# A ring of 24 row slots instead of 16 in both expert passes of a cross-attention and expert-FFN kernel

## The reference

```python
# attention without softmax: 16 heads of 16
kv  = einsum('bthd,bthe->bhde', k, v)          # k, v from the context
att = einsum('bqhd,bhde->bqhe', q, kv) * scale # q from layernorm(x)
x   = x + layer_norm(att + layernorm(x)) * gamma + beta
# expert layer: two of 16 experts per token
t        = layernorm(x)
weights  = softmax(t @ gate_w.T)
w2, idx2 = top_k(weights, 2)
y        = relu(einsum('nh,edh->ned', t, expert_w) + expert_b)
out      = x + sum(y[idx2] * w2)
```

## Time and profile before

| | us |
|---|---|
| time, median of 3 runs | 858.72 (858.34 to 859.48) |
| the profiled execution's own time | 860.73 |
| its span | 859.0 |
| dense half and sorting table, to the first load of pass 0 | 0 to 458.8 |
| pass 0, first to last scatter started | 465.5 to 655.9 |
| pass 1, first to last scatter started | 666.6 to 850.6 |
| end of the span | 859.0 |

### The profile page before, as it was taken

How to read it: one execution, slowest core, us unless ns; L and a number is a source line. 1 busy time by engine, 2 the same in 40 slices (tenths; PEclk the granted TensorE clock), 3 DMA queues, 4 the chain that set the end, 5 groups by cost and what they waited for, 6 DMA issues and landing times. The chain is left out here.

```text
span 859.0 us, 21023 instructions
## 1 busy us (share of the span) xinstructions
PE 752.7 (88%) x5501; PEld 656.9 (76%) x5502; DVE 670.9 (78%) x2218; ACT 593.4 (69%) x1683; POOL 594.6 (69%) x783
## 2 busy tenths in 40 slices
PE   8999999999999999999998777777868799778850
PEld 5887888888888888888875777777765799777740
DVE  5999999999999999999985857777763566555540
ACT  5987999998999999989962545555542577545530
POOL 5575767777777777666663767777674677777774
PEclk9999999999999999999999989999999999999985
DMA  7699988999998877776414889999886999999942
GB/s 200 148 245 309 253 256 246 273 256 251 249 263 249 247 234 224 230 232 224 151 52 152 289 279 304 314 316 310 296 298 224 339 391 385 318 305 321 304 155 73
DMA packets 142885, 218.33 MB, mean 254 GB/s; under 512 B 39103, under 2 KB 74431, under 8 KB 142807
## 3 DMA queue, kind: packets, MB, share of 16 engines
q1 hardware_dynamic: 112999, 131.21, 48.1%
q0 software_dynamic: 29808, 86.20, 32.7%
HBM read 96.36 MB, written 116.80 MB: 248 GB/s over the span
## 5 line engine op out<-in xcount | busy, mean ns | idle before, releaser
L663 POOL DMA_INDIRECT bins<-row_in,put_at x143 | 139.2, 973 | 61.3 <-issue 48.3
L635 POOL DMA_INDIRECT bins<-rows x128 | 130.4, 1019 | 70.6 <-POOL rows L628 47.9
L663 POOL DMA_INDIRECT out_rows<-xh,put_at x143 | 138.9, 971 | 55.8 <-issue 39.4
L742 PE MATMUL ps_q<-h_t,wq 128*128 128x256 f32 x512 | 131.6, 379 | 1.3 <-ACT h_t L970 1.3
L742 PEld LDWEIGHTS ps_q<-h_t,wq 128*128 128x128 f32 x512 | 91.6, 189 | 14.6 <-ACT h_t L970 1.8
L1029 ACT ACTIVATE ps_q<-ps_q,row_in 128x256 f32<-128x256 f32 x144 | 58.6, 445 | 57.2 <-PE ps_q L856 56.7
L854 PE MATMUL ps_q<-we_head,row_head 128*128 x288 | 88.1, 306 | 7.8 <-DVE row_rest L1321 7.8
L537 POOL TENSOR_TENSOR c_rest<-c_sb,c_head 128x240 fp32r<-128x240 f32 x64 | 48.2, 753 | 61.9 <-DVE x L1183 57.3
L612 POOL TENSOR_TENSOR x_beta<-xh,beta_sb 128x512 f32<-128x512 f32 x64 | 85.6, 1338 | 0.8 <-DVE x L1183 0.8
L855 PE MATMUL ps_q<-we_head,row_rest 128*128 x288 | 82.0, 285 | 0.0
L856 PE MATMUL ps_q<-we,row_head 128*128 x288 | 81.9, 285 | 0.0
(11 more groups left out here) (174 smaller groups left out, 2403.2 us busy)
## 6 DMA issues: line engine op xcount, KB each, us to landing
bins<-zeros SPq DMA_DIRECT2D x48, 768.0 KB, 4.6
row_in<-bins SPq DMA_DIRECT2D x128, 260.0 KB
row_in<-bins SPq DMA_DIRECT2D x160, 132.0 KB, 2.1
xh<-in_x SPq DMA_DIRECT2D x64, 256.0 KB, 4.7
c_sb<-in_ctx_t SPq DMA_DIRECT2D x64, 120.0 KB, 4.4
we<-in_we_t SPq DMA_DIRECT2D x8, 512.0 KB, 5.5
we<-be_dram POOLq DMA_DIRECT2D x8, 512.0 KB, 7.8
we<-row_in POOLq DMA_DIRECT2D x8, 512.0 KB, 6.5
```

Of the source, the lines that this page charges most:

```text
L635: pool.indirect_dma_start(out=bins[0], in_=r[:, t, :], out_offset=bass.IndirectOffsetOnAxis(ap=r[:, t, POS_COL:POS_COL + 1].bitcast(I32), ...
L663: pool.indirect_dma_start(out=bins[1] if k == 0 else out, in_=row_in[:, t, :] if k == 0 else y[:, t, :], out_offset=bass.IndirectOffsetOnA ...
L742: mm = pe.matmul(ps_q[dc][:, 0:S], wq[:, c, dc * P:(dc + 1) * P], h_t[:, c, :, :], start=(c == 0), stop=(c == KC - 1))
```

## The change

V goes from 16 to 24, so that a pass has 6 trips instead of 9. `row_in` and `y` have 24 slots each. The room comes from the dense half: `x_sb`, `h`, `x_beta` and `x1` become views of `y`, and `wkv_head` and `wkv_rest` views of `row_head` and `row_rest`, which only the expert passes use. With 12 pairs in a trip there are more scatter semaphores, so others are given up: the expert weights are counted on 2 semaphores instead of 8, and only the first 4 pairs of pass 1 come in two loads, with 4 semaphores. The table's two rows of 128 numbers meet inside the last trip (tiles 120 to 143), so its read is in two instructions. Of the first trip of pass 0, V // 4 is now 6: the first table read is of 6 numbers, the second of 18.

```diff
--- before.py
+++ after.py
@@ -47,7 +47,7 @@
 DUMP = TILES * P
 
 LEAD, FILLS, FACTS = 12, 48, 8
-V = 16
+V = 24
 PAIRS = V // 2
 FILL = TILES // FILLS
 TRIPS = TILES // V
@@ -60,6 +60,7 @@
 SUM_STEP = SLABS + 2
 FIRST_FOLD, FOLD_STEPS = SUM_STEP + 2, 3
 FIRST_HEAD = FIRST_FOLD + FOLD_STEPS
+SPLIT_PAIRS = 4
 RB = 4
 LOG_EXP_SET = 6
 
@@ -139,10 +140,12 @@
 
     def read(k, i, count=V):
 
-        half = int(isinstance(i, int) and i * V >= P)
-        row = (column * 2 + k) * 2 + half
         low = V - count if count > V // 2 else 0
-        eng.load(regs[low:low + count], table[row:row + 1, bass.ds(i * V - half * P + low, count)])
+        cut = min(max(P - i * V - low, 0), count) if isinstance(i, int) else count
+        for half, part in enumerate((slice(low, low + cut), slice(low + cut, low + count))):
+            row = (column * 2 + k) * 2 + half
+            if part.stop > part.start:
+                eng.load(regs[part], table[row:row + 1, bass.ds(i * V - half * P + part.start, part.stop - part.start)])
         return [nc.snap(r, min_val=0, max_val=max_val) for r in regs[low:low + count]]
 
     return read
@@ -178,8 +181,6 @@
         bin_base = sb("bin_base", [P, NT, 2, E])
         base_less = sb("base_less", [P, 2, E])
         eps = sb("eps", [P, 1])
-        wkv_head = sb("wkv_head", [P, KC, 2 * D], F32R)
-        wkv_rest = sb("wkv_rest", [P, KC, 2 * D], F32R)
         wq = sb("wq", [P, KC, D])
         wg = sb("wg", [P, KC, E])
         wg_centred = sb("wg_centred", [P, KC, E])
@@ -198,8 +199,10 @@
         pad_facts = sb("pad_facts", [P, 2, E, ROW - D])
 
 
-        xh = sb("xh", [P, 2, 4 * NT, D])
-        x_sb, h = [xh[:, n].rearrange("p (b t) d -> p b t d", t=NT) for n in range(2)]
+        y = sb("y", [P, V, D])
+        x_sb, h = [y[:, 4 * NT * n:4 * NT * (n + 1)].rearrange("p (b t) d -> p b t d", t=NT) for n in range(2)]
+        x_beta, x1 = [y[:, 8 * NT + 2 * NT * n:8 * NT + 2 * NT * (n + 1)].rearrange("p (b t) d -> p b t d", t=NT)
+                      for n in range(2)]
         c_sb = sb("c_sb", [P, 4, KC, SC])
         c_head = sb("c_head", [P, 2, KC, SC], F32R)
         c_rest = sb("c_rest", [P, 2, KC, SC], F32R)
@@ -209,8 +212,6 @@
         kvm = sb("kvm", [P, KC, P])
         att = sb("att", [P, NT, D])
         scaled = sb("scaled", [P, NT, D])
-        x_beta = sb("x_beta", [P, 2, NT, D])
-        x1 = sb("x1", [P, 2, NT, D])
         rows = sb("rows", [P, 4, NT, ROW])
         h2_t = sb("h2_t", [P, KC, NT, P])
         st = sb("st", [P, 3, 2, NT, 3])
@@ -253,7 +254,8 @@
         put_at = sb("put_at", [P, V], I32)
         row_head = sb("row_head", [P, RB, 2, KC, P], F32R)
         row_rest = sb("row_rest", [P, RB, 2, KC, P], F32R)
-        y = xh[:].rearrange("p a t d -> p (a t) d")[:, 0:V]
+        wkv_head, wkv_rest = [b[:].rearrange("p b t c n -> p (b t c n)")[:, 0:KC * 2 * D]
+                              .rearrange("p (c n) -> p c n", c=KC) for b in (row_head, row_rest)]
 
         ps_ht = ps("ps_ht", [P, KC, NT, P])
         ps_kv = ps("ps_kv", [P, 2 * D])
@@ -281,7 +283,7 @@
         s_wg = sem("gate_weights_loaded")
         s_ident = sem("identity_made")
         s_mask = sem("head_mask_made")
-        s_we = [sem(f"expert_weights_loaded{n}") for n in range(WE_PIECES)]
+        s_we = [sem(f"expert_weight_half{n}_loaded") for n in range(2)]
         s_whead = sem("weight_heads_ready")
         s_wminus = sem("weight_heads_negated")
         s_wrest = sem("weight_rests_ready")
@@ -365,7 +367,7 @@
         s_py = sem("pair_multiplied")
         s_y = sem("pair_result_ready")
         s_loc = sem("second_position_step")
-        s_part = [sem(f"partial_sums_loaded{n}") for n in range(PAIRS)]
+        s_part = [sem(f"partial_sums_loaded{n}") for n in range(SPLIT_PAIRS)]
         s_sum2 = sem("pair_rows_summed")
         s_put = [sem(f"pair_rows_put{n}") for n in range(PAIRS)]
 
@@ -425,7 +427,7 @@
                 for n in pieces(step - 4, 1):
                     sp.dma_start(we[:, :, piece(n)],
                                  we_t.rearrange("(c p) n -> p c n", p=P)[:, :, piece(n)]
-                                 ).then_inc(s_we[n], 16)
+                                 ).then_inc(s_we[n // (WE_PIECES // 2)], 16)
                 if step >= LEAD - 4:
 
                     sp.wait_ge(s_const, 2)
@@ -495,10 +497,12 @@
                     for j in range(PAIRS):
                         sp.wait_ge(s_put[j], put_count(1, 0, j))
                     load_part(0, D, FULL, s_in[0])
-                    for j in range(1, PAIRS):
+                    for j in range(1, SPLIT_PAIRS):
                         load_part(j, D, FULL, s_in[j])
                         load_part(j - 1, 0, D, s_part[j - 1])
-                    load_part(PAIRS - 1, 0, D, s_part[PAIRS - 1])
+                    load_part(SPLIT_PAIRS - 1, 0, D, s_part[SPLIT_PAIRS - 1])
+                    for j in range(SPLIT_PAIRS, PAIRS):
+                        load_part(j, 0, FULL, s_in[j])
                 else:
                     for j in range(PAIRS):
                         sp.wait_ge(s_sum2, pair_number(k, i, j) - PAIRS + 1)
@@ -590,7 +594,7 @@
 
                 if g == 0:
                     pool.wait_ge(s_ebd, 16)
-                pool.wait_ge(s_we[g], 16)
+                pool.wait_ge(s_we[g // (GROUPS // 2)], 16 * WE_PIECES // 2)
                 pool.dma_start(we[:, :, group(g)],
                                be_dram[group(g)].partition_broadcast(P).unsqueeze(1).to_broadcast([P, KC, GROUP * D]),
                                accum_op=ALU.add).then_inc(s_fold[g], 16)
@@ -1353,7 +1357,8 @@
                     sum_tile(j, 0, ps_y[j % YB])
                     at = sum_tile(j, 1, ps_y[j % YB])
                 else:
-                    dve.wait_ge(s_part[j % PAIRS], 32)
+                    if isinstance(number, int) and number < TRIPS * PAIRS + SPLIT_PAIRS:
+                        dve.wait_ge(s_part[j], 32)
                     if not (isinstance(number, int) and number < (TRIPS + 1) * PAIRS):
                         dve.wait_ge(s_put[j % PAIRS], put_count(k, i, j))
                     out_of = ps_y[j % YB]
```

## The result

The kernel became slower by 0.33%: 861.44 us (median of 22 runs) against 858.81 (22 runs of the kernel before beside it), ratio 1.0033, 95% interval 1.0022 to 1.0045. The forecast was 853.2. The profiled execution took 861.95 us, its span 860.2.

What follows compares the result with a forecast made beforehand. The prediction took POOL's list of scatters, about 1.277 us each, as the bound of the expert passes. Its terms: 860.7 - 5.35 - 0.6 + 0.5 = 855.2 profiled, or 858.7 - 5.5 = 853.2 us median; range (8 in 10) 851.4 to 856.6.

Steps and rivals of the forecast that it cites:

- The bound and the ring: POOL's scatters as the limit; 24 slots remove pass 0's stalls after its first trip: -5.35 us, -3.4 at worst.
- The start of pass 0: Pair 2 loaded ahead of SP's second table read, so tile 2 comes earlier: -0.6 us, ends -1.0 and +0.6.
- PE's 24 numbers: PE's first table read grows from 1.30 to about 1.95 us, hidden beside the first row's load: 0, or 0.65 uncovered.
- Pass 1, "the same bytes": Pass 1 keeps its steps; pairs 4 to 11 of the first trip come in one load each instead of two: 0.
- Between the passes: PE's wait before pass 1 grows from 2.33 to some 12 us, delaying its clock's return: +0.5 us, ends 0 and 2.8.
- The clock rival: Half clock after PE's wait before pass 1 costs +2.8 us instead of +0.5; time 855.5; chance 0.10.
- The end: End of pass 1: POOL has more finished tiles before it and its last scatter is as late: 0.
- The longer loop bodies: POOL waits for code at each trip's jump back: slower from 0.55 us each, up to 869; chance 0.07 with address effects.
- The slower outcome: Whole kernel slower than before, through waits for code at trip starts and whatever else moves with addresses; chance 0.07.
- the sum of all bad ends: Whole kernel, every term at its worst: 858.7 - 3.4 + 0.6 + 2.8 + 1 = 859.7 us.

Runs made afterwards that it cites:

- The version with both starts mended: Kernel after (24 slots) with pass 0's table reads of 8 and 16 and 8 pairs of pass 1 in two loads; 854.95 us against 858.95, ratio 0.9963.
- The kernel before with merged loads: Kernel before (16 slots) with pairs 4 to 7 of pass 1's first trip in one load each; 861.48 us against 858.43, ratio 1.0031.

## Why the prediction was wrong

*The bound and the ring: right.* POOL's scatters bound both passes, and 24 slots take away all stalls after the first trip of pass 0. The term was -5.35; from tile 5 of pass 0 to its last scatter the kernel before took 180.6 us, the kernel after 174.5, which is -6.1. The version with both starts mended is faster by 0.37%, 3.2 us by the ratio.

*The start of pass 0: the step that failed.* The prediction priced the second read at 0.94 us, and at 1.79 at worst, from reads of 4, 12 and 16 numbers, all of which start at the first number of the row or a multiple of four behind it. It started at the seventh now and took 3.68. The term was -0.6, with +0.6 as its bad end; from the first scatter to tile 5 it was +3.5 (9.89 to 13.37). In the two profiles the gap before tile 2 shrank by 1.3 (3.63 to 2.30), where up to 1.0 was worked out, but that size is partly luck, as profiles of the unchanged start have 2.34 to 5.38; the gap before tile 4 grew by 4.8 (0.43 to 5.27). The first read, whose two further numbers were put at +0.07, took 0.94 instead of 0.49, and the first scatter came 0.59 later: it starts 10.0 to 10.1 us after the dense half's last in the three profiles with a first read of 4, and 10.4 to 10.9 in the nine with 6 or 8. The Trainium skill's figure of 200 ns a number ("Runtime: NRT & Kernel Launch", Instruction fetch mechanics) was on the table, but was tried on PE's read alone, and set aside because the rows seemed to speak against it; by it SP's 18 numbers take an estimated 3.6. The rows showed only the fast kind of read. PE's 24 numbers start at the first and took 1.82, against 1.95 worked out, so that term was right.

*Pass 1, "the same bytes": the second step that failed.* The prediction put pairs 4 to 11 at 0, because tiles 2 and 4 belong to pairs 1 and 2. It left out, though it had used it for pass 0, that PE transposes two pairs ahead, so that pair 2's products wait for pair 4's rows: +3.0. The kernel before with merged loads shows the cost without the ring. By the table above about 2 us are the order, and the rest is the clock that falls at PE's wait, which the prediction looked for only between the passes.

*Between the passes: right in size.* PE stood for 11.7 us, as forecast some 12:

```profile
657.62 0.69 PE L836 MATMUL ps_ht<-ident,row_in 128*128 128x128 f32 x2 [11.74 <-DMA row_in<-bins]
```

and the first scatter came 0.22 later, against +0.5. The clock rival is ruled out by that, and by eight pairs in two loads, which ends pass 1's gap with PE's wait between the passes left in place.

*The end: left at 0, it was +1.3.* Below.

*The rivals.* The longer loop bodies cost POOL nothing that shows: no gap of more than 0.5 us stands at tiles 24, 48, 72, 96 or 120 of either pass. The slower outcome had been given 0.07, and to another mechanism than the one that came. The two starts (+3.5 and +3.0) took back more than the ring gave, and the end came on top: the time is above even the sum of all bad ends, 859.7, because that sum had no term for pass 1's loads or the end, and too small a one for the read.

## What to carry to other kernels

A longer ring helps only after its first turn; a change of its length also rewrites the first turn, where there is no slack yet, so each load of it has to be placed against the first instruction that waits for it, with the engine's own look-ahead counted in. A price read from a trace holds for the operation in the form that it has there: here a read that starts at the seventh number took about four times what reads with other starts had led to expect.

## What the runs showed of the hardware

A read of numbers from SBUF into registers takes about 0.06 us a number if it starts at the fifth or ninth number of the table's row (12 in 0.75 us, 16 in 0.97), and 0.20 to 0.21 if it starts at the seventh (10, 16 and 18 numbers). From the first, 4 took 0.49, 6 took 0.94 and 8 took 0.73 on SP, 16 took 1.30, 18 took 1.80 and 24 took 1.82 on PE, each at the start of pass 0: a length that is no multiple of four costs as well. Of other starts in the first trips there are only short reads (2 from the 23rd in 0.46, on PE 6 from the 19th in 1.49).

At the end of the program POOL's queue has a row called DRAIN, in the kernel after:

```profile
L160 POOLq DRAIN  x1: 23735/23735/23735, 836.2 to 836.2; - x1
```

and in the kernel before:

```profile
L157 POOLq DRAIN  x1: 22478/22478/22478, 836.3 to 836.3; - x1
```

It ends 8.5 us after the last scatter of the kernel after and 7.2 after that of the kernel before, and the program ends 0.2 us behind it. All seven profiles of kernels with 24 slots have 9.7 us from the last scatter's start to the end of the span, all five with 16 slots 8.4. It does not wait for the scatters to land: SP's list ends with a wait for all of them, and SP reaches its own DRAIN, in the kernel after and in the kernel before, at

```profile
L160 SPq DRAIN  x1: 7/7/7, 853.1 to 853.1; - x1
...
L157 SPq DRAIN  x1: 7/7/7, 853.2 to 853.2; - x1
```

The length of the code written out on POOL is not the cause, and the number of semaphores hardly, since four more for `SPLIT_PAIRS` changed nothing. What it is stays open; it costs the ring of 24 about 1.3 us in every version.
